# Cross attention on one core: where the row maxima are added to the transposed scores, and how far ahead scores are computed

## The reference, cut to what matters

```python
q1, q2 = qh @ wq1, qh @ wq2          # 16 heads of 16 features
k1, k2 = kh @ wk1, kh @ wk2
vp = vh @ wv
s1 = q1 @ k1.T / 4                   # 256 x 256 for each batch and head
s2 = q2 @ k2.T / 4
attn = softmax(s1) - gain * softmax(s2)
o = attn @ vp                        # then normalised over the 16 features of a head
out = o.reshape(B, S, D) @ wo.T
x = layernorm(x + out)
```

## Time and profile before

| | us |
|---|---|
| median of 3 runs | 1679.67 (1678.75 to 1680.36) |
| the profiled execution | 1680.09 |
| its span in the trace | 1678.4 |
| scores of the first item start | 1250.9 |
| last transposed scores (item 63) | 1572.4 |

### The profile page before, as it was taken

How to read it: one execution, slowest core, us unless ns; L and a number is a source line. 1 busy time by engine, 2 the same in 40 slices (tenths; PEclk the granted TensorE clock), 3 DMA queues, 4 the chain that set the end, 5 groups by cost and what they waited for, 6 DMA issues and landing times.

```text
span 1678.4 us, 39380 instructions
## 1 busy us (share of the span) xinstructions
PE 1595.1 (95%) x16590; PEld 1278.9 (76%) x16590; DVE 1264.0 (75%) x2539; ACT 960.2 (57%) x1517; POOL 785.5 (47%) x580
## 2 busy tenths in 40 slices
PE   4799999999999999999999999999989999999998
PEld 3688888888888888888888888888876666666534
DVE  4767778778788778878778778877867777777556
ACT  3466556656555566555566555665436666666545
POOL 3354535535554445534455443544562555553334
PEclk8899999999999999999999999999999999999999
DMA  5100000110001000010001000010077777765001
GB/s 123 52 2 2 33 11 27 33 33 3 9 27 33 33 8 29 2 33 33 11 26 33 2 33 11 27 35 2 2 130 128 139 133 132 135 121 95 1 1 51
DMA packets 71711, 74.29 MB, mean 44 GB/s; under 512 B 18288, under 2 KB 57712, under 8 KB 71536
## 3 DMA queue, kind: packets, MB, share of 16 engines
q1 hardware_dynamic: 71536, 71.78, 20.4%
HBM read 57.08 MB, written 14.68 MB: 43 GB/s over the span
## 4 chain that ended last, share of the span: by engine, by line
PE 79%; DVE 11%; ACT 6%; issue 2%; SPq 0%; POOL 0%; DMA 0%; ACTq 0%; DVEq 0%
PE e_pr L167 9%; PE e_pr L169 7%; PE e_pr L168 7%; PE e_tr L414 6%; PE e_sc L387 5%; PE x_psT L1230 3%; PE e_sc L167 3%; PE e_sc L169 3%; PE e_sc L168 3%; PE e_tr L169 3%; PE e_tr L167 3%; PE e_tr L168 3%; PE x_psO L1249 3%; PE f_bank L1776 3%; PE e_tr L424 3%
## 5 line engine op out<-in xcount | busy, mean ns | idle before, releaser
L689 POOL TENSOR_TENSOR e_h_lo<-e_h_f,e_h_hi 128x512 fp32r<-128x512 f32 x192 | 247.2, 1290 | 301.7 <-ACT e_h_hi L530 299.0
L779 DVE TENSOR_TENSOR e_am<-e_sc,c_amask 128x1024 f32<-128x1024 f32 x192 | 225.6, 1216 | 18.2 <-PE e_sc L387 18.1
L529 ACT ACTIVATE e_h_f<-e_pr,e_h_bias 128x512 f32<-128x512 f32 x192 | 132.1, 688 | 184.8 <-PE e_pr L169 181.1
L1545 DVE TENSOR_REDUCE x_mx<-x_psS 128x4 f32<-128x1024 f32 x128 | 154.9, 1220 | 46.6 <-PE x_psS L1208 46.3
L167 PE MATMUL e_pr<-e_yT_hi,e_W_hi 128*128 128x512 f32 x384 | 168.7, 439 | 0.0
L1380 ACT ACTIVATE x_ex<-x_psT 128x1024 f32<-128x1024 f32 x128 | 131.1, 1025 | 58.3 <-PE x_psT L1234 57.2
L167 PE MATMUL e_tr<-e_W_hi,e_h_hi 128*128 128x256 f32 x576 | 163.0, 283 | 0.0
L168 PE MATMUL e_tr<-e_W_lo,e_h_hi 128*128 128x256 f32 x576 | 160.9, 279 | 0.0
L169 PE MATMUL e_tr<-e_W_hi,e_h_lo 128*128 128x256 f32 x576 | 160.7, 279 | 0.0
L169 PE MATMUL e_pr<-e_yT_hi,e_W_lo 128*128 128x512 f32 x384 | 152.7, 398 | 0.0
L168 PE MATMUL e_pr<-e_yT_lo,e_W_hi 128*128 128x512 f32 x384 | 152.0, 396 | 0.0
(11 more groups left out here) (284 smaller groups left out, 4498.7 us busy)
## 6 DMA issues: line engine op xcount, KB each, us to landing
x_qs<-query_rows SPq DMA_DIRECT2D x128, 128.0 KB, 4.7
e_raw_m<-in_L_attn_W_dram SPq DMA_DIRECT2D x12, 1024.0 KB, 7.2
x_ks<-key_rows SPq DMA_DIRECT2D x64, 128.0 KB, 4.8
query_rows<-x_q_hi SPq DMA_DIRECT2D x16, 256.0 KB, 2.3
query_rows<-x_q_lo SPq DMA_DIRECT2D x16, 256.0 KB, 2.2
x_ctok<-in_ctx_dram SPq DMA_DIRECT2D x8, 256.0 KB, 4.8
x_xo<-in_x_dram SPq DMA_DIRECT2D x8, 256.0 KB, 4.1
key_rows<-x_k_hi SPq DMA_DIRECT2D x8, 256.0 KB, 4.6
```

The costliest lines, as they stand in the source:

```text
L529: act.activation(h_f[:, m % HR, :], ps_pr[m % 2][:, :], ACT.Gelu, bias=h_bias[:, m:m + 1])
L689: pool.tensor_tensor(h_lo[:, m, :], h_f[:, m % HR, :], h_hi[:, m, :].bitcast(F32), ALU.subtract).then_inc(h_lo_done, 1)
L779: dve.tensor_tensor(am[:, s % 2, c, :, :, :], ps_sc[:, :, c * 2 * P:(c + 1) * 2 * P].rearrange("p r (h n) -> p r h n", n=P), amask[:, :].u ...
L1545: dve.tensor_reduce(mx[:, N % 2, :, :].rearrange("p i (a h x) -> p h a i x", h=2, a=2)[:, pair, :, :, 0], ps_s[pair][:, :, :].rearrange("p ...
```

## The change

Four things are done together.

1. **Maxima by DMA.** Of the four 16-row blocks in a half of `qs` and `ks`, three now hold the split queries and keys (the product low by low is gone; `PARTS = ((0, 0, 0), (1, 1, 0), (3, 0, 1))` lists block, query part and key part). The fourth holds, in `ks`, a row of ones and 15 rows of zeros, loaded from an SBUF tile `unit`; in `qs`, zeros, until for each item SP copies the item's four rows of `mT` into one row of each half (`maxima_rows`, two DMAs of two rows of 1 KB). `scores_transposed` then needs no product with `select`.
2. **Scores earlier.** In slot N PE now issues scores(N+2, 1) and scores(N+3, 0), and at the slot's end maxima_transpose(N+2). Items 0, 1 and half of 2 get their scores between the `mlp_down` blocks.
3. **A new order in each slot** on PE, DVE and ACT, the side work at other n; the output projection is split in two; x2's statistics and norm go one batch later.
4. **SP's list by slots**: the stores, loads and maxima rows are interleaved slot by slot.

```diff
+        def maxima_rows(N):
+            b, n = divmod(N, NI)
+            g, k = n // MAPS, n % MAPS
+            wait(sp, rows_set, 32 * N)
+            sp.wait_ge(mT_done, N + 1)
+            for a in range(2):
+                sp.dma_start(qs[b % 2][half_rows(a, 2, 1), 2 * g:2 * g + 2, k, :].bitcast(F32),
+                             mT[2 * a:2 * a + 2, N % 2, :].bitcast(F32)).then_inc(rows_set, 16)
 def stack_keys(e):
+            for a in range(2):
+                sp.dma_start(ks[e % 2][half_rows(a, 2), :, :].bitcast(F32),
+                             unit[0:DH, :].unsqueeze(1).broadcast_to([DH, PAIRS, S])).then_inc(ks_loaded, 16)
             sp.wait_ge(k_stored, 32 * e + 32)
-                for t in range(COPIES):
+                for t, _, low in PARTS:
 def stack_queries(e, c):
+            lanes = DH if e < 2 else 1
+            for a in range(2):
+                sp.dma_start(qs[e % 2][half_rows(a, 2, lanes), pairs, :, :].rearrange("p r k n -> p (r k) n").bitcast(F32),
+                             unit[DH:DH + lanes, :].unsqueeze(1).broadcast_to([lanes, PC * MAPS, S])).then_inc(qs_loaded, 16)
             sp.wait_ge(q_stored, 32 * n + 32)
 # SP, the whole stage
+        for N in range(N_ALL):
+            if after and n == 1:
+                store_keys_hi(e)
+            if after and n == 2:
+                store_keys_lo(e)
+                if e + 1 < B:
+                    load_context(e + 1)
+            if after and n == 3:
+                stack_keys(e)
+                store_queries(e, 0)
+            if after and n == 4:
+                stack_queries(e, 0)
+            if after and n == 5:
+                store_queries(e, 1)
+            if after and n == 6:
+                stack_queries(e, 1)
+            if n == 7 and e + 2 < B:
+                load_input(e + 2)
+            if N + 2 < N_ALL:
+                maxima_rows(N + 2)
 # PE, scores_transposed
             if pair == 0:
-                pe.wait_ge(mT_done, N + 1)
+                pe.wait_ge(rows_set, 32 * N + 32)
...
-                for a in range(2):
-                    mm = pe.matmul(ps_t[:, a, c * S:(c + 1) * S], select[rows, pair, :], mT[rows, N % 2, :],
-                                   start=False, stop=True, skip_group_check=True)
 # PE, the slot of item N
+                scores_transposed(N, 0)
+                if N % 2 == 0:
+                    if N > 0:
+                        attend(N - 1)
+                    if N + 2 < N_ALL:
+                        scores(N + 2, 1)
+                elif N >= 3:
+                    to_tokens((N - 3) // 2)
+                if N % 2 and N + 2 < N_ALL:
+                    scores(N + 2, 1)
+                    if N + 3 < N_ALL:
+                        scores(N + 3, 0)
+                scores_transposed(N, 1)
+                if N % 2 == 0 and N + 3 < N_ALL:
+                    scores(N + 3, 0)
+                side(N)
+                if N % 2:
+                    attend(N - 1)
+                if N + 2 < N_ALL:
+                    maxima_transpose(N + 2)
```

More of the change, by code:

```diff
@@ L471, in _ @@
             cross.queries(0, 1, cross.early(3))
-            for s in range(SB):
-                mlp_down(s, final, L)
+            mlp_down(0, final, L)
+            cross.scores(0, 0)
+            mlp_down(1, final, L)
+            cross.scores(0, 1)
+            mlp_down(2, final, L)
+            cross.maxima(0)
+            cross.scores(1, 0)
+            mlp_down(3, final, L)
+            cross.scores(1, 1)
+            cross.maxima(1)
+            cross.scores(2, 0)
             cross.items()
@@ L1013, in cross_stage @@
     woT = sb_early("woT", [KC, D])
-    first_rows, select = sb_early("first_rows", [2, P]), sb_early("select", [2, P], F32R)
+    unit = sb_early("unit", [S])
     bd = sb_gone("bd", [5 * KC, HC, DH])
@@ L1114, in sync @@
         for c in range(KC):
+            store_queries(0, c)
             stack_queries(0, c)
+        maxima_rows(0)
+        maxima_rows(1)
         load_input(2)
-        for e in range(1, B):
-            if e + 1 < B:
-                load_context(e + 1)
-            stack_keys(e)
-            stack_queries(e, 0)
-            if e + 2 < B:
+        for N in range(N_ALL):
+            b, n, e, d, after, before = slot(N)
+            if after and n == 1:
[14 more added lines that the diff above has]
+            if n == 7 and e + 2 < B:
                 load_input(e + 2)
-            stack_queries(e, 1)
+            if N + 2 < N_ALL:
+                maxima_rows(N + 2)
         follow.sync(sp)
@@ L1183, in out_transpose, with out_project @@
             transpose_to(ps_j, on).then_inc(o_tr, 1)
-        def out_project(d):
+        def out_project(d, parts=range(QB)):
             pe.wait_ge(oT_done, d + 1)
-            for s in range(QB):
+            if 0 not in parts:
+                pe.wait_ge(z_done, QB * d + 1)
+            for s in parts:
                 for c in range(KC):
@@ L1258, in to_tokens, with project_slot, side @@
             mm.then_inc(tok_full, 1)
+        def project_slot(n, after):
+            return n - 6 if after else n - 5
+        def side(N):
+            b, n, e, d, after, before = slot(N)
+            if after and n == 0:
+                pe.wait_ge(q_lo_done, KC * e)
+                wait(pe, z_done, QB * (b - 1))
+                context(e, ps_j)
+            if after and n == 1:
+                x1_transpose(e, ps_j)
+            if after and n == 2:
+                queries(e, 0, ps_j)
+            if after and n == 3:
+                pe.wait_ge(q_lo_done, KC * e + 1)
+                values(e, ps_j)
+            if after and n == 4:
+                pe.wait_ge(v_done, e + 1)
+                queries(e, 1, ps_j)
+            if not after and n < 2 * KC:
+                if n == 0:
+                    pe.wait_ge(q_lo_done, KC * B)
+                    pe.wait_ge(z_done, QB * (B - 2))
+                ffn.rows_in(n // KC, n % KC, ps_j)
+            if before and project_slot(n, after) == -1:
+                if after:
+                    pe.wait_ge(q_lo_done, KC * e + 2)
+                else:
+                    ffn.rows_taken()
+                out_transpose(d)
+            if before and 0 <= project_slot(n, after) < QB:
+                out_project(d, (project_slot(n, after),))
@@ L1336, in items @@
             ffn.stages()
-        return CrossTensor(early, weights, context, values, x1_transpose, queries, items)
+        return CrossTensor(early, weights, context, values, x1_transpose, queries, scores, maxima_transpose, items)
     def scalar(act):
@@ L1449, in x1_norm @@
             rsqrt(1, e)
+            wait(pool, z_done, QB * (e - 2))
             for s in range(QB):
@@ L1493, in items @@
                     encoder_add(b + 2)
-                if before and n == 6:
+                if not after and n == 7:
                     x2_norm(d)
```

225 lines of the change are left out of this document (100 added, 125 removed).

## The result

The changed kernel takes 1776.6 us (1771.4 to 1778.4) against 1680.0: a ratio of 1.057, interval 1.055 to 1.059. The forecast was 1732, the range 1688 to 1758. The direction and the two main waits were right; the time lies 45 us above the forecast and outside the range. The profiled execution took 1771.4 us, 91 more than that of before.

What follows compares the result with a forecast made beforehand. PE was taken as the bound; SP's transfer chain would lengthen batches from 40.0 to 47.8 us. Seven batches +54.6, last batch -4, head +2: +52.6 on 1679.67 gives 1732 us, range 1688 to 1758.

Steps and rivals of the forecast that it cites:

- t4 to the first scores: From slot 4's start (t4) to the next batch's first scores, scores(8, 0) in slot 5: 15.0 us.
- from there to the next slot 0: Rest of the batch after its wait at scores(8, 0): 11.75 us of PE work, 3.5 clock, 0.3 late rows.
- PE work at the full clock: PE's busy time in a batch: 37.85 us less 3.7 for the select products, 34.15.
- clock loss: PE's clock falls to half speed after the long wait in each batch: 3.5 us, bounds 0 and 4.5.
- the chain through SP: Maxima rows, key loads, query stores, then query loads in order on SP; PE waits 9.4 us by scores(8, 0).
- the wait of the next batch's slot 0: Maxima rows of the next item 0, behind six query loads, late by 0 to 1 us; taken as 0.3.
- the last batch: The batch that prepares no other: products saved, its scores of the end already done, -4 us.
- the head: Stage start, scores between the mlp_down blocks wait for loads sooner: +2 us, between -1 and +4.
- stores not held up: Rival: query stores aren't delayed by the key burst; wait 4.35 us, kernel 1671 to 1692; chance 0.08.
- bursts that don't queue: Rival: each transfer lands as a lone one does; wait 2.8 us, batch 37.5, kernel 1658; chance 0.08.
- Clock holds: Rival: PE's clock stays up despite the waits; batch 44.3 us, kernel 1708; chance 0.15.
- No wait at all: Rival: query loads land in time, PE's saving shows in full; batch 35.2 us, kernel 1642; chance 0.04.

Runs made afterwards that it cites:

- the kernel without rows and with late scores: Changed kernel without maxima rows (left out of the computation), next batch's first scores in slot 6 instead of 5, feed-forward loads early: 1660.0 us, ratio 0.989.
- The early loads: Changed kernel with the 15 feed-forward weight and bias loads issued four at a time in the last batch's slots: 1767.4 us, ratio 1.052.
- the same two stores: Changed kernel with the first query half's stores issued in slot 3 ahead of the key loads instead of behind them: 1765.0 us, ratio 1.051.

## Why the prediction was wrong

By its own steps, for a batch (its 47.8 against 51.2 in the windows, 51.6 in the mean of seven). The measured PE work is taken from the kernel without rows and with late scores, which runs at a granted 1.00:

| step | forecast | measured |
|---|---|---|
| slots 0 to 3 | 17.3 | 17.8 |
| t4 to the first scores | 15.0 | 17.7 |
| from there to the next slot 0 | 15.55 | 15.6 |
| PE work at the full clock | 34.15 | 32.3 (64.58 / 2) |
| clock loss | 3.5 | 3.4 (35.7 - 32.3) |
| waits of PE | 10.2 | 15.5 |

**The step that failed is the chain through SP**, "t4 + 15.0": it measured 17.7, which is 2.7 of the 3.8 us a batch. Its order was right, its durations too short. Two maxima rows take 1.17 to 1.29 us to issue, not 0.9. The key loads' issue takes 4.73 for six after 1.68 for two unit loads, 6.4 together (5.3 in most other batches), not 3.6: the price came from the earlier trace rows, where eight went out in 3.63 with nothing in front. The rows of item 4 were out at t4 - 2.8, not - 3.3. The stores, issued at t4 + 3.9 and + 4.3 instead of + 0.3 to + 1.0, landed at t4 + 9.8, not + 7.8, though in 4.9 and 5.4 us rather than the 6.6 of the earlier trace rows. The query loads were issued from t4 + 9.8 on, and the scores that need them started at t4 + 17.7, 7.9 us later and not 7.15. The bound of 11.4 us for this chain's waiting just held the measured 11.4 (5.3 + 6.1).

**A second term was ten times too small**: the wait of the next batch's slot 0 was put at 0.3 and is 2.7 to 4.8. The prediction saw that its pair stands behind six query loads on SP, but let rows land 2.2 to 2.9 us behind their issue; here the product at 1415.78 starts 5.4 us after the pair's issue at 1410.39. It does not show in the third segment, and that is luck: PE's work was put 1.85 too high for the batch, and the clock loss, counted there whole, falls in part in slots 0 to 3. That PE's work fell by more than the selection products is seen with the products kept: 35.9 (71.84 / 2) against 37.85. Most of it is the scores: summed from start to next start, without idle time, they cost 7.0 us a batch before and 5.6 in that kernel, where in each odd slot eight of their products stand in one run. Why that is cheaper stays open. The selection products themselves are then 3.6, as forecast.

**A term was missing**: the tail, +10.3. The text followed SP's list within a batch and not to its end, where the feed-forward's loads stand; counting every DMA behind the added wait would have found them. The early loads take back 2.9 of it in the traces and 9.3 in the medians. The other 7.4 of the traces stay with the new order, to which the prediction gave no cost at the end ("moved side work is the same work").

Right: the two waits with their places, loads issued 10.7 us after the key burst's first load (12.4 after the unit loads' first; forecast 11.1), the clock's fall and its price, the last batch (-4), the head (+2.7 for +2), DVE and ACT no busier. The sizes add up: 3.8 x 7 = 27 in the batches, 10 in the tail and 1 at the head are 38 of the 38.7 by which the profiled execution (+91.3) is over the forecast (+52.6). The remaining 6 of the 45 are the distance of that execution (1771.4) from the median (1776.6), and the 0.4 between execution and median of before.

The rivals: stores not held up, and bursts that don't queue, fall by the 4.9 to 5.4 us of the stores and 5.2 for the key loads (median of those issued after 1434.0). The Trainium skill (DMA: Bandwidth & Descriptors, Anatomy of one DMA) gives the fit that the second goes with for the path of DMAs issued by GpSimd; those here are issued by SP. Three of the rivals' sums (1671 to 1692, 1658, 1642) leave out the head's +2 that the others have. Clock holds falls by the 0.50 windows. "No wait at all" was worth 1642 on paper, 38 less than before; the nearest run without rows gave 1660, and its profiled execution was 22 less. Of the 16 us between, 4 are the head and 8 the tail (113.7 us instead of 106.1), which that rival left at nothing, and only 4 the batches. In the batches the next bound shows: PE is idle 3.6 us of 35.9, and its longest sum of waits stands at the transposed maxima, which wait for DVE's reductions. In the stage:

```profile
PE x_psS L1270 <- DVE x_mx L1611: 13.8, 22, 1.8
PE x_psS L1263 <- issue: 6.8, 7, 1.7
```

So the selection products' 3.6 us of PE work were worth 1.5 a batch (12.2 us over eight in the medians; 16.9 between the two stages in the traces) once the waits for transfers were gone.

## What to carry to other kernels

Follow an in-order DMA list to its end before adding an item that waits for compute: everything behind it, up to the next stage's weights, is now paced by that compute. Be wary of a small transfer that an engine needs within about a slot while bursts are under way, on whichever queue it is issued; here the whole saving of the products was 1.5 us a batch, and the transfers that replaced them cost 3.7 to 4.3 at best and 12 as written. When an edit helps in one setting, test it again once the bound has moved: the same two stores were worth -12 us in the kernel after and +14 to +38 in the kernels with late scores. And take a cause from a run only after listing all that the run changed: the one with cut bursts had also moved the stores back.

## What the runs showed of the hardware that was not expected

- Issuing was slower right behind other large loads: six query loads after a wait take 2.67 us on SP, six key loads right behind two unit loads of 128 KB 3.9 to 4.9, and in the kernel that leaves those two out 2.7 to 3.7. The issuing itself became a term of the chain. What slows it is not shown.
- A 2 KB DMA between SBUF tiles takes 0.6 us to issue, on SP or on ACT (1.16 to 1.29 a pair), more than the 0.45 of a 128 KB load from DRAM: its small size made it no cheaper.
- One wait of 4.2 to 6.2 us in a batch, as in the kernel without rows, cost 1.9 us of clock besides itself (34.2 us of PE busy a batch at a mean granted 0.90, against 32.3 at 1.00 in the kernel without rows and with late scores).
